# Sparse first FFN: what GpSimd does between its sends, and the tick at which the expert blocks begin

## The chip, the core and the metric

The kernel runs on one core of a Trainium2 chip. The metric is the device time in microseconds (us), lower is better. Three runs of the kernel before gave 2142.99, 2148.42 and 2147.09 us (median 2147.09).

The core has these engines, each with its own in-order program: TensorE (PE in the profile; its weight loads are PEld), VectorE (DVE), ScalarE (ACT), GpSimd (POOL) and SyncE (SP), which here only issues DMAs. They wait for each other by semaphores.

## The reference, cut to what matters

The input is eight rows (sequences) of 1024 tokens with 256 numbers each. Three parts follow one another, each added to `x`:

```python
x = x + 0.5 * ffn(layernorm(x))      # first FFN: the part that is changed
x = x + attention(layernorm(x))      # light windows of 64 and 256 heavy tokens
x = x + 0.5 * ffn(layernorm(x))      # second FFN, dense in this kernel

def ffn(x):                          # 8 experts, two for each token
    logits = x @ router_w + router_b
    w, idx = top_k(softmax(logits), 2);  w = w / sum(w)
    h = gelu(x @ W1[e] + b1[e])      # 256 -> 128, for each expert e
    y = h @ W2[e] + b2[e]            # 128 -> 256
    return sum over the token's two experts of w * y
```

With two experts the normalized weights depend only on the difference of the two largest logits: with t = exp(second - first), they are 1/(1+t) and t/(1+t).

## The kernel before, in words

The first FFN is sparse. Each row is routed; every token's normalized 256 numbers are sent by two scattering DMAs to spots in DRAM (`spots_d`), so that the tokens of one expert lie together; then blocks of 256 tokens are loaded, run through one expert's two products, and stored (`made_d`). Attention's first steps fetch the results back. Rows are taken in three batches, (0, 1), (2, 3, 4) and (5, 6, 7), with 23, 31 and 31 blocks, 85 in all. A batch's blocks need all of its rows sent and a table of its counts.

All five engine programs of this stage run over the same ticks `tau`; a tick is no clock, it is only the order in which each engine takes its work. `ROW_AT` gives each row the tick at which it begins, `STEP0` the tick of block 0, and block s is at tick `STEP0 + s`. A row's stages, by ticks after its start:

- 0 and 1, DVE: `bn_stats` and `bn_aggr` of the two halves (`row_stats`, needs the row's load)
- 2, POOL: the norm factors (`row_rstd`), four operations, one of them a power
- 3 and 4, ACT: the normalization in place (`row_norm`, L1127)
- 4 to 7: turning on PE (L816), copies on ACT (L1136), logits on PE (L826), copies on ACT (L1143), turning the logits (L833)
- 8, DVE: ranks of the experts (`row_route`, L1422 to L1443)
- 9, PE: counts before each token (L841, L843). 9, POOL: exp of the difference by a power (`row_exp`, L1915)
- 10, DVE: the spots (`row_spots`, L1476), the batch's table after its last row, and the two gates (`row_gates`)
- 11 to 16, POOL: 16 indirect DMAs (`send`, L1923), 128 tokens of 1 KB each

A block's stages: load by SP three ticks ahead (L604, into one of four buffers `xin`, so a load waits until the block four before it has been turned), at its tick the turning on PE (L853), the copy of its expert's W1 (L1164) and the copy `xh` (L1149) on ACT; one tick later the first product (L862), two later Gelu (L1170), three later the second product (L877), four later the bias add on DVE (L1538), five later the store (L610). Before the first block of a batch SP writes eight pads of zeros (`pads`, L592, 256 KB each), and waits for the batch's sends and for the pads to land.

There are four buffers `xb` for rows: the load of row r (`row_load`, L585) is issued five ticks ahead of the row and waits until row r-4 has been sent. SP also writes spare zeros for each batch (L652, 7 x 256 KB) at ticks 12, 40 and 64. Attention's preparation of row 0 (fetching, norms, turning) is tied to `ROW0 = STEP0 + FIRST[2] + 1`, where `FIRST[2]` is 54, and runs beside the blocks of the last batch. `made`, `sent` and the stores' semaphores close the stage; attention follows, unchanged.

Of the kernel before, what the change touches and what calls it, by code (L numbers as in the profile page):

```python
# [18 lines left out]
P = 128  # L19
# [19 lines left out]
def build(nc, x_in, gamma_h, wq_h, wkv_h, wo_h, ln_g, ln_b, wqkv, wo_l, rt_q, rt_kv,  # L39
# [30 lines left out]
    with ctx:  # L70
# [111 lines left out]
        half_a, euler_a = sb("half_a", [P, T]), sb("euler_a", [P, T])  # L182
        st_a, mv_a = sb("st_a", [P, T, 6]), sb("mv_a", [P, T, 2])
        vt_a, rs_a, nm_a = sb("vt_a", [P, T]), sb("rs_a", [P, T]), sb("nm_a", [P, T])
        chosen = [sb(f"chosen{i}", [P, T + 1, E], BF16) for i in range(2)]
        lg = sb("lg", [P, T, E])
        lmax_a, t2nd_a, wt_a = sb("lmax_a", [P, T]), sb("t2nd_a", [P, T]), sb("wt_a", [P, T])
# [89 lines left out]
        s_abn, s_amv, s_avar, s_ars, s_arstd, s_anorm = sem("a_bn"), sem("a_mv"), sem("a_var"), sem("a_rs"), sem("a_rstd"), sem("a_normed")  # L277
        s_ax, s_lq, s_ra, s_exa, s_pos, s_tab, s_zero = sem("xa_turned"), sem("logits_left"), sem("route_a"), sem("exp2_a"), sem("spots"), sem("table"), sem("pads")
        s_home, s_b2all, s_xa0 = sem("homes"), sem("b2_all"), sem("xa_ld_first")
# [37 lines left out]
        STEP0 = 26  # L317
        TICKS = STEP0 + STEPS + 6
        ROW_AT = (0, 6, 12, 19, 26, 36, 46, 56)
# [217 lines left out]
        NA, NPOS, NTAB = 14, 6, 16  # L537
# [36 lines left out]
        def sp_program():  # L574
# [60 lines left out]
            for tau in range(TICKS):  # L635
                for s_ in step_at(tau - 5):
                    block_store(s_)
                for s_ in step_at(tau + 3):
                    block_load(s_)
                for r in row_at(tau + 5, 0):  # L640
                    if r >= 4:
                        row_load(r)
                if tau == 8:
                    sp.dma_start(wqkv_st[:, :, :], wqkv.rearrange("(c p) n -> p c n", p=P)).then_inc(s_wld[4], 16)
                if tau == 10:
                    sp.dma_start(b2_all[:, :, :].rearrange("p e n -> p (e n)"), b2.rearrange("(a e) n -> a (e n)", a=1).broadcast_to([P, E * D])).then_inc(s_b2all, 16)
                if tau in (12, 40, 64):

                    if tau == 12:
                        sp.wait_ge(s_const, CONST)  # L650
                    n = (12, 40, 64).index(tau)
                    sp.dma_start(spots_d[n][SPARE[n]:SPARE[n] + (E - 1) * BLK, :].rearrange("(j p s) d -> p j (s d)", p=P, s=BT),  # L652
                                 zeros[:, :, :].rearrange("p s d -> p (s d)").unsqueeze(1).broadcast_to([P, E - 1, BT * D])).then_inc(s_spare, 16)
                if tau == 18:

                    sp.wait_ge(s_wlo, 6)
                    sp.dma_start(w1_d, w1_s[:, :, :, :, :].rearrange("p e w c f -> p (e w c f)").bitcast(F32)).then_inc(s_wst, 16)
                    for n in range(2):
                        sp.dma_start(w2_d[n], w2_s[n][:, :, :].rearrange("p e n -> p (e n)").bitcast(F32)).then_inc(s_wst, 16)
                    sp.dma_start(b2_d, b2_s[:, :].bitcast(F32)).then_inc(s_wst, 16)  # L660
                if tau == 74:
                    attn_load(0, x_v)
                if tau == 100:
                    sp.dma_start(wqh_s[:, :, :], wq_h.rearrange("(c p) n -> p c n", p=P)).then_inc(s_late, 16)
                    sp.dma_start(wol_s[:, :, :], wo_l.rearrange("(c p) n -> p c n", p=P)).then_inc(s_late, 16)
                if tau == 106:
                    sp.dma_start(wkvh_s[:, :, :], wkv_h.rearrange("(c p) n -> p c n", p=P)).then_inc(s_late, 16)
                    sp.dma_start(woh_s[:, :, :], wo_h.rearrange("(c p) n -> p c n", p=P)).then_inc(s_late, 16)
# [400 lines left out]
        def act_program():  # L1069
# [52 lines left out]

            def row_norm(r, h):
# [195 lines left out]
            for tau in range(TICKS):  # L1319
                for s_ in step_at(tau - 2):  # L1320
                    block_gelu(s_)
                for s_ in step_at(tau):
                    w1_copy(s_)
                    block_x(s_)
                for h in range(2):
                    for r in row_at(tau, 3 + h):
                        row_norm(r, h)
                for what in tick_jobs(tau):
                    evac(*what)
# [10 lines left out]
                if 14 <= tau < 14 + 2 * 3 * C and tau % 2 == 0:  # L1340
                    i, n = (tau - 14) // 2 % C, (tau - 14) // 2 // C * INNER
                    split(wqkv_s[0][:, i, n:n + INNER], wqkv_st[:, i, n:n + INNER], (s_wld[4], 16))
# [33 lines left out]
        def dve_program():  # L1376
# [22 lines left out]
            def row_stats(r, h):  # L1399
# [9 lines left out]
                if h == 0 and r > 0:  # L1409
                    dve.wait_ge(s_avar, 2 * r)  # L1410
# [4 lines left out]
            def row_route(r):  # L1415
# [25 lines left out]
                dve.tensor_reduce(t2nd_a[:, :], l2nd[:, :, :], AX_X, ALU.add).then_inc(s_ra)  # L1441
                dve.wait_ge(s_ra, n + 10)
                dve.tensor_tensor(t2nd_a[:, :], t2nd_a[:, :], lmax_a[:, :], ALU.subtract).then_inc(s_ra)  # L1443

            def row_gates(r):
                n = NA * r
                dve.wait_ge(s_exa, r + 1)
                g = share[:, r, :, :]
                dve.tensor_scalar(wt_a[:, :], t2nd_a[:, :], 1.0, 2.0, ALU.add, ALU.mult).then_inc(s_ra)
                dve.wait_ge(s_ra, n + 12)  # L1450
                dve.reciprocal(g[:, 0, :], wt_a[:, :]).then_inc(s_ra)
                dve.wait_ge(s_ra, n + 13)
                dve.tensor_tensor(g[:, 1, :], t2nd_a[:, :], g[:, 0, :], ALU.mult).then_inc(s_ra)
# [319 lines left out]
            for tau in range(TICKS):  # L1773
                for s_ in step_at(tau - 4):
                    block_left(s_)
                for h in range(2):
                    for r in row_at(tau, h):
                        row_stats(r, h)
                for r in row_at(tau, 10):
# [3 lines left out]
                    row_gates(r)  # L1783
# [13 lines left out]
                if 15 <= tau < 15 + 2 * 3 * C and tau % 2 == 1:  # L1797
                    m = (tau - 15) // 2
# [50 lines left out]
        def pool_program():  # L1849
# [49 lines left out]
            def row_rstd(r):  # L1899

                pool.wait_ge(s_amv, 2 * r + 2)
                if r > 0:
                    pool.wait_ge(s_anorm, 4 * r)
                    pool.wait_ge(s_arstd, r)
                pool.tensor_scalar(vt_a[:, :], mv_a[:, :, 1], LN_EPS, None, ALU.add).then_inc(s_avar)
                pool.tensor_scalar(nm_a[:, :], mv_a[:, :, 0], -1.0, None, ALU.mult).then_inc(s_avar)
                pool.wait_ge(s_avar, 2 * r + 1)
                pool.tensor_tensor(rs_a[:, :], vt_a[:, :], half_a[:, :], ALU.pow).then_inc(s_ars)
                pool.wait_ge(s_ars, r + 1)
                pool.wait_ge(s_avar, 2 * r + 2)  # L1910
                pool.tensor_tensor(nm_a[:, :], nm_a[:, :], rs_a[:, :], ALU.mult).then_inc(s_arstd)
# [71 lines left out]
            pool.memset(half_a[:], -0.5)  # L1983
            pool.memset(euler_a[:], float(np.e))
# [30 lines left out]
            for tau in range(TICKS):  # L2015
                for r in row_at(tau, 2):
                    row_rstd(r)
                for r in row_at(tau, 9):
                    row_exp(r)
# [93 lines left out]
```

## Time and profile before

| what | us |
|---|---|
| median of three runs | 2147.09 |
| the profiled execution's own time | 2143.95 |
| its span | 2142.2 |
| PE busy | 1899.1 (89% of the span) |
| DVE busy | 1389.8 (65%) |
| ACT busy | 1175.3 (55%) |
| POOL busy | 1126.9 (53%) |
| SP's load of row 1 for attention, behind the last block's store, at | 417.7 |

The page's slices of 53.6 us each show the first FFN in the first eight: PE is busy there 3 to 8 tenths, and 8 or more tenths in nearly all that follow. The granted TensorE clock is below full speed in the first seven of them.

```profile
PE   4377877968998998998998998998999999999998
PEclk8678988989999999999999999999999999999999
DMA  8557576611031031031031031030023111111110
```

### The profile page before, as it was taken

The page shows a single profiled execution, that of the slowest core. Times are in us where ns is not written, and L with a number is a line of the kernel's source. Part 1 is how long each engine was busy: PE and PEld are TensorE (multiplying, and loading weights), DVE is VectorE, ACT ScalarE, POOL GpSimd, SP SyncE. Part 2 cuts the span into 40 slices and gives each one's busy share as a digit, 9 for nine tenths or more (in the row PEclk, how much of TensorE's full clock was granted, in tenths as well). Part 3 has the DMA queues.
Part 4 walks back from the last instruction along what each step waited for, and adds up shares of the span by engine and source line. Part 5 has one row for each costly group of instructions (what it writes and reads, how often), then busy time and mean ns, then how long its engine had stood idle before and what let it go on. Part 6 is the DMA issues. An engine that isn't in the chain of part 4 may idle for free.

```text
span 2142.2 us, 37969 instructions
## 1 busy us (share of the span) xinstructions
PE 1899.1 (89%) x11764; PEld 1409.7 (66%) x11764; DVE 1389.8 (65%) x4781; ACT 1175.3 (55%) x2936; POOL 1126.9 (53%) x1253
## 2 busy tenths in 40 slices
PE   4377877968998998998998998998999999999998
PEld 2155566845665666665665665665676688888887
DVE  5343344476586585685685685685664488888887
ACT  4244444645557556556556556656555555555554
POOL 5745434157277277377376386386354444444444
PEclk8678988989999999999999999999999999999999
DMA  8557576611031031031031031030023111111110
GB/s 291 194 170 260 197 255 231 233 57 33 1 94 40 1 97 38 1 97 38 1 102 33 1 104 31 3 105 28 1 58 116 37 33 38 40 41 39 36 36 30
DMA packets 106575, 173.64 MB, mean 81 GB/s; under 512 B 13296, under 2 KB 64904, under 8 KB 105480
## 3 DMA queue, kind: packets, MB, share of 16 engines
q1 hardware_dynamic: 83336, 118.42, 16.7%
q0 software_dynamic: 20736, 52.52, 7.8%
q8 instruction: 97, 1.59, 0.3%
q14 instruction: 102, 0.84, 0.1%
q10 hardware_dynamic: 2304, 0.28, 0.1%
HBM read 80.33 MB, written 90.84 MB: 80 GB/s over the span
## 4 chain that ended last, share of the span: by engine, by line
PE 46%; DVE 16%; issue 13%; POOL 12%; ACT 8%; DMA 2%; another core or an unknown queue 1%; SPq 1%; DVEq 0%; ACTq 0%; POOLq 0%
PE bank L720 6%; PE bank L722 5%; PE bank L721 5%; PE bank L1009 4%; PE bank L998 4%; PE bank L969 4%; PE bank L980 4%; PE bank L940 3%; POOL spots_d L1923 3%; ACT prob L1292 2%; POOL prob L1970 2%; DVE x L1550 2%; DVE st L1381 2%; PE bank L971 1%; PE bank L877 1%
## 5 line engine op out<-in xcount | busy, mean ns | idle before, releaser
L1970 POOL TENSOR_TENSOR prob<-prob,rden 128x512 f32<-128x512 f32 x320 | 337.2, 1055 | 452.7 <-DVE rden L1756 449.1
L1292 ACT ACTIVATE prob<-prob,nmax 128x256 f32<-128x256 f32 x512 | 256.0, 502 | 401.8 <-DVE nmax L1738 393.4
L1738 DVE CUSTOM_DVE_ANT_0 prob<-bank,mask 128x256 f32<-128x256 f32 x512 | 195.4, 418 | 105.0 <-PE bank L969 103.5
L1625 DVE SCALAR_TENSOR_TENSOR xb<-bank,gate,xb 128x256 f32<-128x256 f32 x512 | 211.9, 477 | 55.6 <-PE bank L722 55.1
L969 PE MATMUL bank<-kT,qT 64*128 64x256 f32 x1024 | 213.2, 434 | 22.2 <-DVE nmax L1738 21.6
L1885 POOL TENSOR_TENSOR hl<-hf,hh 128x512 fp32r<-128x512 f32 x128 | 164.6, 1291 | 113.9 <-ACT hh L1109 109.2
L980 PE MATMUL bank<-ident,prob 128*128 128x128 f32 x1280 | 199.3, 279 | 20.7 <-POOL prob L1970 20.7
L980 PEld LDWEIGHTS bank<-ident,prob 128*128 128x128 f32 x1280 | 153.9, 142 | 79.9 <-POOL prob L1970 33.3
L1750 DVE COPY probT<-bank 128x512 f32<-128x512 f32 x160 | 110.2, 688 | 117.5 <-PE bank L980 116.6
L1108 ACT ACTIVATE hf<-bank,b1s 128x512 f32<-128x512 f32 x128 | 88.2, 689 | 171.2 <-PE bank L722 167.7
L998 PE MATMUL bank<-probT,V 128*64 128x128 f32 x2048 | 170.7, 288 | 9.1 <-ACT oT_s L1308 7.7
L1538 DVE TENSOR_TENSOR yout<-bank,b_all 128x512 f32<-128x512 f32 x85 | 58.0, 690 | 174.4 <-remote 71.5
L1957 POOL DMA_INDIRECT hs_d<-yr,place x128 | 129.8, 1014 | 44.5 <-issue 32.8
L969 PEld LDWEIGHTS bank<-kT,qT 64*128 64x128 f32 x1024 | 94.9, 188 | 86.5 <-issue 48.2
L998 PEld LDWEIGHTS bank<-probT,V 128*64 128x64 f32 x2048 | 108.8, 137 | 64.4 <-issue 61.0
L1923 POOL DMA_INDIRECT spots_d<-xb,spot x128 | 125.2, 978 | 48.1 <-issue 36.3
L720 PE MATMUL bank<-w,hh 128*128 128x256 f32 x512 | 146.4, 286 | 3.8 <-POOL hl L1885 2.7
L722 PE MATMUL bank<-w,hh 128*128 128x256 f32 x512 | 144.8, 283 | 0.0
L721 PE MATMUL bank<-w,hl 128*128 128x256 f32 x512 | 144.4, 282 | 0.0
L1009 PE MATMUL bank<-wol,oT_s 128*128 128x256 f32 x512 | 126.3, 390 | 1.2 <-ACT xf_t L1239 1.2
L1770 DVE TENSOR_TENSOR x<-bank,x 128x256 f32<-128x256 f32 x64 | 27.1, 423 | 145.3 <-PE bank L1009 145.3
L877 PE MATMUL bank<-w_st,hf 128*128 x340 | 97.0, 411 | 21.3 <-issue 13.6
(254 smaller groups left out, 5016.7 us busy)
## 6 DMA issues: line engine op xcount, KB each, us to landing
xin<-spots_d SPq DMA_DIRECT2D x85, 256.0 KB
made_d<-yout SPq DMA_DIRECT2D x85, 256.0 KB
x<-in_L_attn_x SPq DMA_DIRECT2D x8, 1024.0 KB
x_d<-x SPq DMA_DIRECT2D x8, 1024.0 KB, 4.4
xb<-x_d SPq DMA_DIRECT2D x16, 512.0 KB, 3.8
out<-xb SPq DMA_DIRECT2D x16, 512.0 KB, 2.9
xb<-in_L_attn_x SPq DMA_DIRECT2D x7, 1024.0 KB
spots_d<-zeros SPq DMA_DIRECT2D x24, 256.0 KB
```

The lines of the kernel that those rows point to most:

```text
L720: pe.matmul(o, w[0], x[0], start=start, stop=False)
L721: pe.matmul(o, w[1], x[0], start=False, stop=False)
L722: return pe.matmul(o, w[0], x[1], start=False, stop=stop)
L969: ins = pe.matmul(bank[g % NS][:, 0:KEYS], qT[hs, hp, t * P:(t + 1) * P], kT[hs, hp, t * P:t * P + KEYS], start=True, stop=True)
L980: ins = pe.transpose(bank[3 + j % 2][:, (2 * h + kk) * P:(2 * h + kk + 1) * P], prob[j % NP][:, h, kk * P:(kk + 1) * P], ident[:, :])
L998: ins = pe.matmul(bank[5][h * DH:(h + 1) * DH, hp * P:(hp + 1) * P], V[:, t + kk, hs] if t < T else hv[:, kk, hs], probT[j % 2][:, 2 * h + ...
L1009: ins = pe.matmul(bank[tb][:, 0:D], oT_s[:, ch, :], w[:, ch, :], start=(ch == 0), stop=(ch == HC - 1))
L1292: act.activation(prob[j % NP][:, h, :], src, ACT.Exp, bias=nmax[:, j % 4, h:h + 1], scale=-1.0 if light else 1.0, accum_out=den[:, j % 4, ...
L1625: dve.scalar_tensor_tensor(out=x, in0=bank[ob][:, (t % 2) * D:(t % 2 + 1) * D], scalar=gate[:, k % 2, t, e:e + 1], in1=x, op0=ALU.mult, op ...
L1738: ins = dve.tensor_tensor_reduce(prob[j % NP][:, h, :], bank[g % NS][:, 0:KEYS], mask[:, which, :], -1.0, 3e38, ALU.add, ALU.min, nmax[:, ...
L1923: pool.indirect_dma_start(spots_d[batch_of_row(r)], bass.IndirectOffsetOnAxis(spot[:, r, c, t:t + 1], 0), xb[r % 4][:, t, :], None).then_i ...
L1970: pool.tensor_tensor(prob[j % NP][:, :, :], prob[j % NP][:, :, :], rden[:, j % 4, :].unsqueeze(2).broadcast_to([P, 2, KEYS]), ALU.mult).th ...
```

## The change

1. `row_rstd` moves from POOL to ACT: one `Ln` with bias eps and one `Exp` with scale -0.5 give the factor; the shift is one operation on DVE (`row_shift`).
2. `row_exp` and `row_gates`, once for each row, become one `Exp` over all rows on ACT at tick 51 (`share_exps`) and three operations on DVE at tick 52 (`shares`). The first combine of attention waits for them.
3. POOL then has nothing between its sends.
4. Rows begin every six ticks, and block 0 is at tick 44 (before: 26), two ticks after row 7 has begun. Loads for attention move from ticks 74, 100, 106 to 94, 120, 126; the splits of `wqkv` are at every tick instead of every second one.

```diff
-        STEP0 = 26
+        STEP0 = 44
-        ROW_AT = (0, 6, 12, 19, 26, 36, 46, 56)
+        ROW_AT = (0, 6, 12, 18, 24, 30, 36, 42)
+        SHARES = ROW_AT[-1] + 9
-        NA, NPOS, NTAB = 14, 6, 16
+        NA, NPOS, NTAB = 11, 6, 16
...
+            def row_rstd(r):
+                act.wait_ge(s_amv, 2 * r + 2)
+                act.activation(ln_a[:, :], mv_a[:, :, 1], ACT.Ln, bias=eps_a[:, 0:1]).then_inc(s_aln)
+                act.wait_ge(s_aln, r + 1)
+                if r > 0:
+                    act.wait_ge(s_arstd, r)
+                act.activation(rs_a[:, :], ln_a[:, :], ACT.Exp, scale=-0.5).then_inc(s_ars)
+            def share_exps():
+                act.wait_ge(s_ra, NA * ROWS)
+                act.activation(t2nd_a[:, :, :], t2nd_a[:, :, :], ACT.Exp).then_inc(s_exa)
...
+                for r in row_at(tau, 2):
+                    row_rstd(r)
...
+                if tau == SHARES:
+                    share_exps()
...
-            def row_gates(r):
-                dve.wait_ge(s_exa, r + 1)
...
+            def row_shift(r):
+                dve.wait_ge(s_ars, r + 1)
+                if r > 0:
+                    dve.wait_ge(s_anorm, 4 * r)
+                dve.scalar_tensor_tensor(out=nm_a[:, :], in0=mv_a[:, :, 0], scalar=-1.0, in1=rs_a[:, :], op0=ALU.mult, op1=ALU.mult).then_inc(s_arstd)
+            def shares():
+                dve.wait_ge(s_exa, 1)
+                dve.tensor_scalar(wt_a[:, :, :], t2nd_a[:, :, :], 1.0, 2.0, ALU.add, ALU.mult).then_inc(s_share)
...
+                    dve.wait_ge(s_share, 3)
...
-            def row_rstd(r):
-                pool.wait_ge(s_amv, 2 * r + 2)
...
-                pool.tensor_tensor(rs_a[:, :], vt_a[:, :], half_a[:, :], ALU.pow).then_inc(s_ars)
...
-            def row_exp(r):
-                pool.wait_ge(s_ra, NA * r + 11)
-                pool.tensor_tensor(t2nd_a[:, :], euler_a[:, :], t2nd_a[:, :], ALU.pow).then_inc(s_exa)
```

What the change does to the order of the engines shows at three places: GpSimd's sends, SyncE ahead of the first block, and TensorE and ScalarE at block 0. On GpSimd before, from the first row's sends on (`xb_194` and the numbers after it are the row buffers; a number at the end counts equal operations):

```order
L1915 TENSOR_TENSOR t2nd_a<-euler_a,t2nd_a 128x8
L1923 DMA spots_d<-xb_194,spot 20224x256 x9
L1905 TENSOR_SCALAR vt_a<-mv_a 128x8
L1906 TENSOR_SCALAR nm_a<-mv_a 128x8
L1908 TENSOR_TENSOR rs_a<-vt_a,half_a 128x8
L1911 TENSOR_TENSOR nm_a<-nm_a,rs_a 128x8
L1923 DMA spots_d<-xb_194,spot 20224x256 x3
```

and now, where the row buffers are `xb_193` to `xb_196`:

```order
L1934 DMA spots_d<-xb_193,spot 20224x256 x16
L1934 DMA spots_d<-xb_194,spot 20224x256 x16
L1934 DMA spots_d<-xb_195,spot 28416x256 x16
L1934 DMA spots_d<-xb_196,spot 28416x256 x16
L1934 DMA spots_d<-xb_193,spot 28416x256 x16
L1934 DMA spots_d<-xb_194,spot 28416x256 x16
L1934 DMA spots_d<-xb_195,spot 28416x256 x16
L1934 DMA spots_d<-xb_196,spot 28416x256 x16
```

The eight operations on norm factors and exps that stood between the sends of each row are gone, and the 128 sends stand in one piece.

On SyncE before, from the load of row 4 to the first block's load:

```order
L585 DMA xb_194<-in_L_attn_x 128x8x256 [waits sent0]
L714 TENSOR_LOAD pad_row_179 [waits table]
...
L592 DMA spots_d<-zeros 128x512
L714 TENSOR_LOAD block_row_176 [waits pads,spare_zero,sent1,sent0]
L604 ISA
L604 DMA xin_164<-spots_d 128x512
```

and now:

```order
L586 DMA xb_193<-in_L_attn_x 128x8x256 [waits sent0]
L586 DMA xb_194<-in_L_attn_x 128x8x256 [waits sent1]
L586 DMA xb_195<-in_L_attn_x 128x8x256 [waits sent2]
L586 DMA xb_196<-in_L_attn_x 128x8x256 [waits sent3]
L653 DMA spots_d<-zeros 128x7x512
L715 TENSOR_LOAD pad_row_178 [waits table]
...
L593 DMA spots_d<-zeros 128x512
L715 TENSOR_LOAD block_row_175 [waits pads,spare_zero,sent1,sent0]
L605 ISA
L605 DMA xin_163<-spots_d 128x512
```

The loads of rows 5, 6 and 7 and the second batch's spare zeros have moved ahead of the first batch's pads and of every block's load.

On TensorE now, around block 0 (`xin_163` is its load, `chosen_133` belongs to row 6):

```order
L834 MATMUL bank<-ident,lgT_167 128x8 x4
L834 MATMUL bank<-ident,lgT_168 128x8 x4
L854 MATMUL bank<-ident,xin_163 128x128 x4
L854 MATMUL bank<-ident,xin_164 128x128 x4
L863 MATMUL bank<-xh_198,w_now_189 128x256 x2
L842 MATMUL bank<-chosen_133,later 128x72
L844 MATMUL bank<-chosen_133,ones 128x64
```

Before, in this place row 3 was routed:

```order
L853 MATMUL bank<-ident,xin_164 128x128 x4
L833 MATMUL bank<-ident,lgT_168 128x8 x4
L833 MATMUL bank<-ident,lgT_169 128x8 x4
L853 MATMUL bank<-ident,xin_165 128x128 x4
L862 MATMUL bank<-xh_199,w_now_190 128x256 x2
L853 MATMUL bank<-ident,xin_166 128x128 x4
L862 MATMUL bank<-xh_200,w_now_191 128x256 x2
L841 MATMUL bank<-chosen_135,later 128x72
```

Row 6's counts now stand behind the turning of blocks 0 and 1, and all of row 7's work on TensorE behind that; before, this was so from row 3 on.

On ScalarE now, at tick 44:

```order
L1164 ACTIVATE xh_198<-bank 128x512
L1127 ACT_TABLE_LOAD
L1127 ACTIVATE ln_a<-mv_a,eps_a 128x8
L1131 ACT_TABLE_LOAD
L1131 ACTIVATE rs_a<-ln_a 128x8
```

Row 7's factors stand behind block 0's copy, and each of the eight rows brings two table loads.

## Rows read from the trace of the kernel before

**Rows 1.** Line L1149 (copy `xh`, one a block) by stretches; x counts blocks
```profile
core 0: us, ACT busy (x), PEclk, DMA share, GB/s
86.90:131.20 44.30, 3.54 (x6) 0.77 0.58 191
131.20:160.00 28.80, 4.08 (x7) 0.80 0.38 128
160.00:178.50 18.50, 1.77 (x3) 0.86 0.97 345
178.50:196.50 18.00, 3.51 (x6) 0.91 0.44 149
196.50:221.00 24.50, 1.75 (x3) 0.84 0.85 283
221.00:243.20 22.20, 4.11 (x7) 0.87 0.47 151
243.20:267.30 24.10, 2.33 (x4) 0.93 0.64 218
267.30:278.30 11.00, 2.90 (x5) 1.00 0.78 286
278.30:301.00 22.70, 1.75 (x3) 0.79 0.64 220
301.00:321.70 20.70, 5.28 (x9) 0.90 0.86 272
321.70:328.80 7.10, 0.58 (x1) 0.78 0.50 168
...
348.00:411.70 63.70, 16.42 (x27) 0.99 0.78 259
```

**Rows 2.** GpSimd's groups in the first 320 us
```profile
L1923 POOL DMA_INDIRECT spots_d<-xb,spot x128 | 125.2, 978 | 48.1 <-issue 36.3 <-DVE spot L1476 11.8
L1915 POOL TENSOR_TENSOR t2nd_a<-euler_a,t2nd_a 128x8 f32<-128x8 f32 x8 | 14.2, 1772 | 70.0 <-DVE t2nd_a L1443 69.8
L1908 POOL TENSOR_TENSOR rs_a<-vt_a,half_a 128x8 f32<-128x8 f32 x8 | 13.6, 1706 | 0.0
```

**Rows 3.** GpSimd in order of time: start, duration, what
```profile
35.07 1.23 POOL L1923 DMA_INDIRECT spots_d<-xb,spot  x1 [0.20 <-issue]
...
103.85 0.51 POOL L1905 TENSOR_SCALAR vt_a<-mv_a 128x8 f32<-128x8 f32 x1
...
145.56 1.67 POOL L1915 TENSOR_TENSOR t2nd_a<-euler_a,t2nd_a 128x8 f32<-128x8 f32 x1 [15.53 <-DVE t2nd_a L1443]
```

**Rows 4.** SyncE in order of time
```profile
61.29 0.40 SPq L585 DMA_DIRECT2D xb<-in_L_attn_x  x1
62.41 15.65 SPq L592 DMA_DIRECT2D spots_d<-zeros  x8
86.88 24.71 SPq L604 DMA_DIRECT2D xin<-spots_d  x8
```

**Rows 5.** ScalarE in order of time: copies of blocks 0, 1 and 53, a table load
```profile
90.85 0.58 ACT L1149 ACTIVATE xh<-bank 128x512 f32<-128x512 f32 x1
...
106.72 0.60 ACT L1149 ACTIVATE xh<-bank 128x512 f32<-128x512 f32 x1 [14.98 <-remote]
107.33 1.28 ACT L1170 ACT_TABLE_LOAD   x1
108.63 0.47 ACT L1170 ACTIVATE hf<-bank,b1s 128x256 f32<-128x256 f32 x1
...
322.38 0.58 ACT L1149 ACTIVATE xh<-bank 128x512 f32<-128x512 f32 x1
```

**Rows 6.** VectorE in order of time: spots of row 0, route of row 3
```profile
34.33 0.17 DVE L1476 CAST spot<-spot_f 128x16 uint32<-128x16 f32 x1
...
103.18 0.22 DVE L1422 TENSOR_TENSOR lg<-bank,rbs 128x64 f32<-128x64 f32 x1 [12.63 <-remote]
```

**Rows 7.** TensorE in order of time: the turned logits of row 3
```profile
90.23 0.66 PE L833 MATMUL bank<-ident,lgT 8*128 8x8 f32 x8
```

More of the change, by code:

```diff
@@ L1339, in act_program @@
                         act.activation(b2_s[at_:at_ + E, :], b2_st[:, :], ACT.Copy).then_inc(s_whi)
-                if 14 <= tau < 14 + 2 * 3 * C and tau % 2 == 0:
-                    i, n = (tau - 14) // 2 % C, (tau - 14) // 2 // C * INNER
+                if 14 <= tau < 14 + 3 * C:
+                    i, n = (tau - 14) % C, (tau - 14) // C * INNER
                     split(wqkv_s[0][:, i, n:n + INNER], wqkv_st[:, i, n:n + INNER], (s_wld[4], 16))
@@ L1409, in row_stats @@
                 if h == 0 and r > 0:
-                    dve.wait_ge(s_avar, 2 * r)
+                    dve.wait_ge(s_aln, r)
                 for q in range(TG * h, TG * h + TG):
@@ L1440, in row_route @@
                 dve.wait_ge(s_ra, n + 8)
-                dve.tensor_reduce(t2nd_a[:, :], l2nd[:, :, :], AX_X, ALU.add).then_inc(s_ra)
+                dve.tensor_reduce(t2nd_a[:, r, :], l2nd[:, :, :], AX_X, ALU.add).then_inc(s_ra)
                 dve.wait_ge(s_ra, n + 10)
-                dve.tensor_tensor(t2nd_a[:, :], t2nd_a[:, :], lmax_a[:, :], ALU.subtract).then_inc(s_ra)
-            def row_gates(r):
-                n = NA * r
-                dve.wait_ge(s_exa, r + 1)
[L1448 to L1453, printed above, removed]
+                dve.tensor_tensor(t2nd_a[:, r, :], t2nd_a[:, r, :], lmax_a[:, :], ALU.subtract).then_inc(s_ra)
+            def row_shift(r):
[6 more added lines that the diff above has]
+                dve.tensor_scalar(wt_a[:, :, :], t2nd_a[:, :, :], 1.0, 2.0, ALU.add, ALU.mult).then_inc(s_share)
+                dve.wait_ge(s_share, 1)
+                dve.reciprocal(share[:, :, 0, :], wt_a[:, :, :]).then_inc(s_share)
+                dve.wait_ge(s_share, 2)
+                dve.tensor_tensor(share[:, :, 1, :], t2nd_a[:, :, :], share[:, :, 0, :], ALU.mult).then_inc(s_share)
             def row_spots(r):
@@ L1778, in dve_program @@
                         row_stats(r, h)
+                for r in row_at(tau, 2):
+                    row_shift(r)
+                if tau == SHARES + 1:
+                    shares()
                 for r in row_at(tau, 10):
@@ L1782, in dve_program @@
                         batch_table(batch_of_row(r))
-                    row_gates(r)
                 for r in row_at(tau, 8):
@@ L1796, in dve_program @@
                     split(b2_s[64:64 + E, :], b2_st[:, :], b2_s[0:E, :], 7)
-                if 15 <= tau < 15 + 2 * 3 * C and tau % 2 == 1:
-                    m = (tau - 15) // 2
+                if 15 <= tau < 15 + 3 * C:
+                    m = tau - 15
                     i, n = m % C, m // C * INNER
@@ L2015, in pool_program @@
             for tau in range(TICKS):
[L2016 to L2019, printed above, removed]
                 for i in range(2 * T):
```

28 lines of the change are left out of this document (9 added, 19 removed).

## The prediction

> **What bounds the kernel now.** The first FFN ends at 417.7 us of the span (SyncE's load of row 1 for attention), and everything behind it is unchanged work that starts when the last blocks are done. So the change is worth what it does to that point. I read the slices of the page first: TensorE is busy 89% of the whole span, but in the first eight slices only 3 to 8 tenths, at a granted clock of 0.5 to 0.9. The slack is there. Then I counted blocks: ScalarE's copy L1149 runs once for each block, so its count by stretches is the pace of the pipeline [rows 1]. I cut the stretches where GpSimd starts and stops sending.
>
> In the five stretches in which GpSimd sends while blocks run (those that begin at 86.9, 160.0, 196.5, 243.2 and 278.3) there are 6+3+3+4+3 = 19 blocks in 44.3+18.5+24.5+24.1+22.7 = 134.1 us: 7.06 us a block. In the five between them 7+6+7+5+9 = 34 blocks take 28.8+18.0+22.2+11.0+20.7 = 100.7 us: 2.96 a block with the routing of rows among them, and 2.30 where no row is routed (9 in 20.7, from 301.0). The last stretch has 27 in 63.7, 2.36 [rows 1]. So a block costs three times as much beside sends, and blocks 0 to 53 take from 90.85 to 322.38 [rows 5], 231.5 us.
>
> What stalls there is seen best at the start. Row 3's turned logits are recorded on TensorE at 90.23 [rows 7], yet VectorE, which waits for nothing else, gets them at 103.18 [rows 6]; block 1's copy on ScalarE starts at 106.72 after 14.98 us idle [rows 5]. GpSimd's sends pause at 103.85, for row 4's norm factors [rows 3]. The other slow stretches end within 2 to 3 us of the last send too. I do not know what TensorE waits for; I use only that it goes with sends. The granted clock of 0.77 to 0.86 in these stretches and 0.99 to 1.00 in steady ones [rows 1] follows from the idle time.
>
> **Part by part.** *GpSimd.* It loses 8 x 1.77 = 14.2 us of exps and 8 x 1.71 = 13.6 us of powers and the small operations around them [rows 2]. A send is 0.978 us and 36.3/123 = 0.30 of issue behind it [rows 2], together 1.27, so a row takes 16 x 1.27 = 20.3 us and eight rows 162 us without a pause. The first send waits now for the spots, done at 34.33 + 0.17 = 34.5 [rows 6], instead of the power until 35.07 [rows 3]: 0.4 us, on the path of the sends. Row 3's last send ends at 34.7 + 4 x 20.3 = 116. Row 6 could begin at 34.7 + 6 x 20.3 = 156.
>
> *SyncE.* All rows' loads now stand ahead of the first pads. Row 7's load waits for row 3 sent, 116 and about 1.5 for landing: 117.5. Behind it come 1.0 MB of row, 1.8 MB of spare zeros and 2.1 MB of pads before a block may be loaded. Before, 1.0 + 2.1 MB took from 61.29 to 86.88, 25.6 us [rows 4], part of it waiting for row 1 to be sent. Bounds for the new 4.9 MB: 14 us at 345 GB/s, the highest rate in [rows 1], and 25.6 x 4.9 / 3.1 = 40 us. I take 22 us (some 225 GB/s, between the 191 and 283 of two stretches with sends). Block 0 loads at 139.5 and is copied 4.0 us later, as before (86.88 to 90.85 [rows 4, 5]): 143.5, against 90.85.
>
> *Blocks beside sends.* Rows 0 to 5 are routed by then, row 6 up to its logits. Row 6's counts stand behind the turning of blocks 0 and 1 and one hidden product, and row 7's factors behind block 0's copy. From 143.5 until 156 row 5's sends run; then GpSimd runs dry, TensorE is free of the stall, row 6 is ready near 158. In 14.5 us at 7.06: 2 blocks. Row 6's sends and their tail, 158 to 180: 22/7.06 = 3 blocks. Row 7 is then routed in its last ticks (46 to 52 stand between blocks) and GpSimd idles, as it does now (15.53 us ahead of row 4's exp [rows 3]); I take 10 us, 4 blocks. Row 7's sends, 190 to 212: 3 blocks. So 12 blocks by 212.
>
> *The rest.* 42 blocks to block 53, with no send and no row beside them: 42 x 2.30 = 96.6. The change of batch costs 7.1 - 2.3 = 4.8 (one block in 7.1, from 321.7 [rows 1]). Two table loads around the single exp at tick 51 (Exp in, Gelu back) are 2 x 1.28 [rows 5] = 2.6, of which the slack of ScalarE in a step hides a part: 1.9. Sum 212 + 96.6 + 4.8 + 1.9 = 315.3, against 322.4: 7 us earlier. Bounds of the pace of the 42: 2.17 would be the shortest spacing within the last stretch as a whole (I take 2.2) and 2.96 the mean with rows: 309 to 343.
>
> *At nothing.* The 16 table loads of the rows (two a row, by the order of ScalarE) are 20.5 us of ScalarE, and 14 of them lie in the time in which it waits for sends to free a row buffer; if that cover were gone they would cost 2.6 us a row in the chain of each. Row 0's chain: 4 operations on GpSimd and one table load before, two loads and three small ones now, equal within 1 us. The gates of all rows together are four small operations long before attention's first combine. The wqkv splits at every tick are done before the blocks; so are, by then, all waits on them. The last batch, 322 to 418, keeps its own order of blocks, fetches and loads, and shifts as a whole; if its cover changed it would cost or give what lies in its 19.2 us beside fetches, some 5 us.
>
> One rule weighs against this. [Rows 5] show a table load of 1.28 us, with the activation behind it 1.30 us after its start. The Trainium skill ("ScalarE: Activation LUTs", "What ACT_TABLE_LOAD costs") adds a drain of about 1.38 us to each, 2.66 in all. By it the pair at tick 51 would be 5.3 us and the sum would end about 2.7 us later; the trace does not show the drain, so I keep the row.
>
> Result: the profiled execution's 2143.95 - 7 = 2137; on the median of the runs, 3.1 above it, 2140.
>
> **The rivals.**
>
> *A: sends are not the cause.* The slow stretches also hold loads of rows (1 MB each, ahead of blocks in SyncE's queue), and TensorE's work of a row; these are what goes from the blocks' time. For it: each slow stretch has a row under way. Against: the ends fall on GpSimd's pauses. Then blocks beside sends go at 2.96: 23 by 212, and 31 x 2.3 + 6.7 behind them: 290, 32 us earlier, 2108 on the median. With only half of it 2124.
>
> *B: slower, by a long run of sends.* Before, GpSimd's own norm operations broke the runs (5 us at 103.85, when blocks 1 to 3 slipped through); now nothing does. If TensorE stands while sends run, block 0's late load and the stall hold row 6's counts and row 7's whole chain. Priced: pads at the upper bound, block 0 copied at 158 when GpSimd has run dry; row 6 spots at 163; 1 block beside its sends until 185; row 7's chain then takes 19 us, 6 blocks; its sends until 226, 2 blocks: 10 blocks by 226, 44 x 2.3 + 6.7: 334, 12 us later, 2159 at the outside and 2155 as the case's centre. It decides at 3 blocks fewer than my 12 by 212. A rule gives the same end: by the Trainium skill ("DMA: Bandwidth & Descriptors", "Queues, rings and completion order") a completion is a strongly ordered write that lands only after every earlier write of that DMA engine, across its queues, so block loads would complete behind scattered sends. [Rows 6, 7] show a wait of 13 us that is on no DMA at all, so the rule alone does not cover it.
>
> *C: it does little.* The blocks begin 53 us later and the rest is 2.4 to 2.5 a block because of spare zeros and a second change of buffers: 42 x 0.15 = 6 us more. Then it ends within 0.3%, near 2146.
>
> **How the numbers follow.** My forecast 0.42, A 0.20, B 0.24, C 0.14. The bound of no change is 0.3%, 6.4 us, about what a measurement of this kernel can tell. The forecast's own range is 2128 to 2150, of which 0.28 is faster by more than the bound, 0.12 within it and 0.02 slower. A is faster. C is 0.12 within and 0.02 slower; B 0.02 within and 0.22 slower. Faster 0.48, same 0.26, slower 0.26. The range 2110 to 2158 takes A nearly whole and B to its centre and beyond.
>
> **What would show it right or wrong.** GpSimd's sends stand at 1.27 us apart from 34.7 to 156 without a gap, then a gap of some us before row 6 and one of about 10 before row 7, the last send near 210. The first block load at 139.5 (135 to 155). L1149's count is about 9 between 143 and 190 and 12 by 212, then one each 2.3 us at a clock near 1.0. Row 7's first norm is behind block 0's copy. Block 53 is copied near 315, attention's load of row 1 near 411. Twenty-one table loads instead of four, and no time behind 411 that differs. I am wrong in the mechanism if blocks beside sends go at 3 us, or if the stretch behind the last send has gaps of its own; in the size, if the first load is far from 139.5 or row 7's gap far from 10.

## The result and the profile after

The changed kernel takes 2182.36 us (median of 4 runs, 2180.86 to 2184.63), against 2147.76 for the kernel before, timed beside it: a ratio of 1.0163, interval 1.0141 to 1.0185. It is 35 us slower; the forecast was 7 us faster, with 2110 to 2158 as its range. The profiled execution took 2182.36, its span 2180.6.

From the page, the span and two of the slices' rows (columns as before):

```profile
span 2180.6 us, 37947 instructions
...
PE   3335787978899898998999998998999999999998
...
PEclk8657799989999999999999999999999999999999
```

TensorE is busy 3 to 5 tenths in the second to fourth slice (55 to 218 us), where it was 3 to 7 before. The count of blocks tells more. Copies of blocks on ScalarE (L1164 now, L1149 in [rows 1]) by stretches, cut again where GpSimd starts and stops sending:

```profile
core 0: us, ACT busy (x), PEclk, DMA share, GB/s
37.00:79.30 42.30, 0.00 (x0) 0.66 0.61 223
79.30:94.00 14.70, 0.00 (x0) 0.50 0.24 80
94.00:134.40 40.40, 0.00 (x0) 0.58 0.37 127
134.40:153.10 18.70, 0.00 (x0) 0.59 0.78 273
153.10:186.10 33.00, 0.00 (x0) 0.68 0.35 120
186.10:253.70 67.60, 7.13 (x12) 0.79 0.49 162
253.70:276.00 22.30, 5.60 (x10) 0.87 0.71 225
276.00:294.00 18.00, 1.98 (x4) 0.81 0.86 304
294.00:355.50 61.50, 16.19 (x28) 1.00 0.77 250
355.50:385.00 29.50, 2.95 (x5) 0.78 0.69 227
385.00:446.90 61.90, 15.89 (x26) 0.99 0.80 257
```

The 12 blocks beside sends are there, but by 253.7 us instead of 212. Behind them block 53 is copied at 355.5, so the stretch with no send took 101.8 us, where my sum had 103.3. Between 294.0 and 355.5 a block takes 61.5/28 = 2.20 us. The loss has been made by the time the last send is out, and measured by my forecast it all lies ahead of block 0: from block 0's copy at 186.1 to the last send the 12 blocks take 67.6 us, where my forecast had 68.5 (143.5 to 212).

GpSimd in order of time: where rows' sends stop and start, and its group in the first 320 us ([rows 2, 3] are the same of before):

```profile
36.95 1.27 POOL L1934 DMA_INDIRECT spots_d<-xb,spot  x1 [30.04 <-DVE spot L1501]
...
78.30 0.96 POOL L1934 DMA_INDIRECT spots_d<-xb,spot  x1 [0.30 <-issue]
93.99 0.96 POOL L1934 DMA_INDIRECT spots_d<-xb,spot  x1 [14.73 <-DVE spot L1501]
...
133.38 0.96 POOL L1934 DMA_INDIRECT spots_d<-xb,spot  x1 [0.30 <-issue]
153.08 0.96 POOL L1934 DMA_INDIRECT spots_d<-xb,spot  x1 [18.74 <-DVE spot L1501]
...
233.45 0.95 POOL L1934 DMA_INDIRECT spots_d<-xb,spot  x1 [11.66 <-DVE spot L1501]
```

```profile
L1934 POOL DMA_INDIRECT spots_d<-xb,spot x128 | 125.9, 983 | 120.8 <-DVE spot L1501 83.6 <-issue 37.2
```

A send is what it was (0.983 us and 0.29 of issue). But GpSimd now waits 83.6 us for spots, 30.04 of them ahead of row 0. The other 53.6 are five gaps between rows (14.7, 18.7, 4.1, 4.3 and 11.7 us), and I had put two there, together 12 us. Before, it waited 11.8 us for spots and 69.8 for what its exps read [rows 2], nearly as long, and had 34 us of own work besides. The engine that was to be relieved stands still, because the rows are not routed.

Why not, row 2 shows. ScalarE in order of time: it copies row 2's turned tiles (L1151) and logits (L1158), then makes row 3's factors:

```profile
53.30 0.60 ACT L1151 ACTIVATE xa<-bank 128x512 f32<-128x512 f32 x1 [1.47 <-PE bank L817]
56.88 0.60 ACT L1151 ACTIVATE xa<-bank 128x512 f32<-128x512 f32 x1 [2.98 <-remote]
...
61.15 0.60 ACT L1151 ACTIVATE xa<-bank 128x512 f32<-128x512 f32 x1 [3.15 <-remote]
66.09 0.60 ACT L1151 ACTIVATE xa<-bank 128x512 f32<-128x512 f32 x1 [4.35 <-PE bank L827]
...
75.27 0.59 ACT L1158 ACTIVATE lgT<-bank 8x512 f32<-8x512 f32 x1 [8.07 <-remote]
83.01 0.59 ACT L1158 ACTIVATE lgT<-bank 8x512 f32<-8x512 f32 x1 [7.15 <-remote]
...
84.65 1.28 ACT L1127 ACT_TABLE_LOAD   x1
85.94 0.30 ACT L1127 ACTIVATE ln_a<-mv_a,eps_a 128x8 f32<-128x8 f32 x1
86.26 1.28 ACT L1131 ACT_TABLE_LOAD   x1
```

TensorE in order of time, the logits of row 2 and their turning:

```profile
61.89 3.39 PE L827 MATMUL bank<-xa,rw_st 128*8 128x512 f32 x4 [3.18 <-issue]
66.84 1.88 PE L827 MATMUL bank<-xa,rw_st 128*8 128x512 f32 x4 [1.56 <-issue]
83.65 1.02 PE L834 MATMUL bank<-ident,lgT 8*128 8x8 f32 x8 [14.93 <-ACT lgT L1158]
```

TensorE's last logits product is done at 68.7 by the record; ScalarE, idle, copies it at 83.01. The trace also records each update of a semaphore. For the six groups of row 2, the end of the matmul that increments the semaphore and the time at which the semaphore moved (us, from the trace's records, not from a view of the page):

```
matmul ends   semaphore moves   behind   ScalarE starts
  52.26           53.28           1.02       53.30
  53.17           56.86           3.69       56.88
  55.13           61.12           5.99       61.15
  58.71           66.07           7.36       66.09
  65.27           75.25           9.98       75.27
  68.71           82.98          14.27       83.01
```

ScalarE starts 0.02 to 0.03 us behind each update. TensorE itself goes on: ScalarE's copy of 66.09 is done at 66.69, and the matmuls that need it start at 66.84, 8.4 us before the increment of the group ahead of them moves (75.25). What is late is TensorE's increment, and the later the longer GpSimd has been sending without a break; the last send of this run starts at 78.30. In the same stretch (37 to 254 us) 80 updates by ScalarE's own instructions are recorded, none more than 0.1 us behind its end; of TensorE's 72, 31 are. This is what [rows 5 to 7] showed without a name: a product recorded at 90.23 and received at 103.18.

### The profile page after: what moved, and what is told of

Read it like the earlier page. It is cut to its first block, busy times and chain, and to the rows that moved or that the text cites. A ratio compares the mean times of both kernels' runs of the same rounds, so it can differ in the third digit from the quotient of the medians.

```text
span 2180.6 us, 37947 instructions
## 1 busy us (share of the span) xinstructions
PE 1898.9 (87%) x11764; PEld 1412.9 (65%) x11764; DVE 1389.5 (64%) x4768; ACT 1203.1 (55%) x2970; POOL 1094.4 (50%) x1212
## 4 chain that ended last, share of the span: by engine, by line
PE 50%; DVE 16%; issue 13%; ACT 8%; POOL 8%; DMA 3%; another core or an unknown queue 1%; SPq 1%; ACTq 0%; DVEq 0%; POOLq 0%
PE bank L721 6%; PE bank L723 5%; PE bank L722 5%; PE bank L1010 4%; PE bank L999 4%; PE bank L970 4%; PE bank L981 3%; PE bank L878 3%; PE bank L941 3%; PE bank L863 3%; ACT prob L1307 2%; POOL prob L1981 2%; DVE x L1576 2%; DVE st L1400 1%; PE bank L972 1%
## 5 line engine op out<-in xcount | busy, mean ns | idle before, releaser
L1934 POOL DMA_INDIRECT spots_d<-xb,spot x128 | 125.9, 983 | 120.8 <-DVE spot L1501 83.6
L999 PEld LDWEIGHTS bank<-probT,V 128*64 128x64 f32 x2048 | 108.7, 137 | 64.4 <-issue 60.9
L721 PE MATMUL bank<-xt_hi,wqkv_hi 128*128 128x512 f32 x256 | 114.8, 448 | 0.0
```

Source lines behind the costliest of these rows:

```text
L721: pe.matmul(o, w[0], x[0], start=start, stop=False)
L999: ins = pe.matmul(bank[5][h * DH:(h + 1) * DH, hp * P:(hp + 1) * P], V[:, t + kk, hs] if t < T else hv[:, kk, hs], probT[j % 2][:, 2 * h + ...
```

## The experiments

In what follows "late" counts, while sends run, TensorE's increments that land over 0.1 us behind the latest matmul that could have made them. It is a lower bound: a queue of increments can hide part of it. Some updates are missing from each trace (one of TensorE's semaphores has 545 for 568 matmuls in the changed kernel). Where sends are called a run, no other operation of GpSimd and no gap lies between them. An increment is put to the last send that started before it landed, if that was at most 4 us before.

### One part of the change at a time

**ticks_only**: the kernel before, with the new numbers.

```diff
-        STEP0 = 26
+        STEP0 = 44
-        ROW_AT = (0, 6, 12, 19, 26, 36, 46, 56)
+        ROW_AT = (0, 6, 12, 18, 24, 30, 36, 42)
```

(and SyncE's three late loads 20 ticks later, as in the change)

> The kernel before with only the numbers of ticks changed (blocks begin at tick 44, rows at 0, 6, 12, 18, 24, 30, 36, 42; the norm factors and exps stay on GpSimd). Theory 1, the late start is the cost: few blocks run beside the sends, as in the changed kernel (14 by 259 us against 36 before), so the stage is 25 to 40 us longer and the time 2172 to 2190. Theory 2, GpSimd's lost work is the cost (its norm operations broke the runs of sends and let the next row's routing through): with them back the rows are routed faster and the time is within 0.5% of the kernel before, 2140 to 2158. In both, TensorE's semaphore increments land late beside sends (up to 14 us in the changed kernel).

Measured: 2162.56, ratio 1.0065 (1.0048 to 1.0082), 14 us slower than before and 20 faster than the changed kernel. It lies between the two theories. The sends end at 233 (253 in the changed kernel) although GpSimd has 34 us more to do. GpSimd in this run, around the factors of row 3:

```profile
72.22 0.96 POOL L1923 DMA_INDIRECT spots_d<-xb,spot  x1 [0.30 <-issue]
73.26 0.25 POOL L1905 TENSOR_SCALAR vt_a<-mv_a 128x8 f32<-128x8 f32 x1
...
73.80 1.67 POOL L1908 TENSOR_TENSOR rs_a<-vt_a,half_a 128x8 f32<-128x8 f32 x1
...
75.92 1.07 POOL L1923 DMA_INDIRECT spots_d<-xb,spot  x1 [0.17 <-issue]
...
79.56 1.67 POOL L1915 TENSOR_TENSOR t2nd_a<-euler_a,t2nd_a 128x8 f32<-128x8 f32 x1
81.42 1.03 POOL L1923 DMA_INDIRECT spots_d<-xb,spot  x1 [0.19 <-issue]
```

The increments of TensorE's matmuls that end at 78.05, 79.03, 81.54 and 82.39, just behind the two breaks, land within 0.02 us. The rows' sends then start 25 us apart (33.9, 60.9, 86.6, 111.0, 136.1, ...), with a single longer gap, 9.7 us between two sends' starts, at 199. The work that the change takes off GpSimd was what let the routing through.

**engine_only**: the changed kernel, with the old numbers (the reverse of the diff above).

> The changed kernel with the ticks of before (blocks from tick 26, rows at 0, 6, 12, 19, 26, 36, 46, 56): GpSimd only sends, ScalarE makes factors and gates. Theory 1 (the late start is the cost): 2125 to 2150, no slower than before, since blocks run beside the sends again and the sends end up to 28 us earlier. Theory 2 (the unbroken sends are the cost): 2165 to 2185, with gaps of 10 us and more between the rows' sends as in the changed kernel.

Measured: 2159.02, ratio 1.0050 (1.0032 to 1.0068), 11 us slower than before. So neither theory alone: late start 14 us, GpSimd's breaks 11 (with ScalarE's table loads and splits, which this kernel has too), and the remaining 9 to 10 of the 35 only with both. From row 2 on, a row's first send starts 12, 12, 15, 26, 27 and 25 us behind the last one of the row before; the last send is at 310.0, later than the 297.5 of before. Of the increments that land from the sixth send of a run on, 51 of 53 are late, up to 15.6 us; at the first to fifth 1 of 18. Blocks by stretches (L1164), with sends and without:

```profile
102.40:313.00 210.60, 25.81 (x44) 0.86 0.62 204
313.00:424.40 111.40, 24.12 (x40) 0.92 0.77 249
```

### What holds the increments

**pause_each**: the changed kernel; the edit is behind the send in `send`, twice:

```diff
+                pool.wait_ge(s_idle, idles[0])
+                pool.tensor_tensor(idle_b[:, :], euler[:, :], euler[:, :], ALU.pow).then_inc(s_idle)
+                idles[0] += 1
```

> The changed kernel with two small powers on GpSimd behind each send, so that sends stand some 3 us apart instead of 1.27. If TensorE's increments are held by sends that come back to back, they land within 1 us now, no row waits for its spots behind TensorE, and blocks beside sends go at 2.2 to 3.5 us instead of 7; the stage is then bound by GpSimd, 128 sends at 3 us, and the whole is some 2250 to 2350. If it is each send that costs TensorE a fixed time, the increments are as late per send as now: a block beside sends takes the time of one or two sends and more, and the time is longer still.

Measured: 2299.07, sends 3.4 us apart. All 183 increments that land in the time of the sends are in time, 43 of them while a send is under way, and blocks 0 to 53, all beside sends, go at 2.7 us each. So a send by itself costs TensorE nothing; only sends in a run do.

**plain_send**: each send a plain transfer by the same engine. The blocks read a buffer whose rows are not sorted, so the output is another.

```diff
-                pool.indirect_dma_start(spots_d[batch_of_row(r)], bass.IndirectOffsetOnAxis(spot[:, r, c, t:t + 1], 0), xb[r % 4][:, t, :], None).then_inc(s_sc[r % 4], 16)
+                pool.dma_start(plain_d[(16 * r + i) * P:(16 * r + i + 1) * P, :], xb[r % 4][:, t, :]).then_inc(s_sc[r % 4], 16)
```

> The changed kernel with each send a plain transfer of the same 128 x 1 KB by GpSimd, to a buffer of its own, instead of an indirect one (blocks then read that buffer: the rows are not sorted by expert, so the result is another). If the indirect addressing is what holds TensorE's increments, they are on time (under 0.1 us) and blocks beside sends go at 2.2 to 3 us. If it is any transfer whose descriptors GpSimd writes, or the bytes, they stay late by up to 14 us and the stage is like that of the changed kernel.

Measured: 2093.42, with sends 0.53 us apart. Between 35 and 169 us 90 increments of TensorE land and none is late. But 16 such sends are out in 8.5 us, and indirect ones hold nearly every increment only from the sixth, over 6 us into a run. Time and form were not told apart; plain_double, below, does it.

**plain_double**: plain_send, with a second transfer ahead of each (128 x 1 KB from a tile of zeros, to a buffer of its own).

```diff
+                pool.dma_start(extra_d[(16 * r + i) * P:(16 * r + i + 1) * P, :], zeros[:, 0, :]).then_inc(s_extra, 16)
```

> plain_send with every send preceded by a second plain transfer of the same size, from a tile of zeros to a buffer of its own, so that GpSimd issues 32 transfers a row, 0.54 us apart, in runs of 17 us. In plain_send the runs were 16 long and 8.5 us, and of the increments that landed beside them none was late, but indirect sends hold increments only from the sixth of a run, 7.6 us in: time and number are not told apart. If it is the time for which GpSimd issues without a break, increments are late here by several us from 8 us into a run, as beside indirect sends. If it is the indirect form, none is late even at 17 us.

Measured: 2120.61. The rows came so close together that the first run is 96 transfers in 51 us; GpSimd at its end:

```profile
86.59 0.54 POOL L1939 DMA_DIRECT2D extra_d<-zeros  x1
87.12 0.54 POOL L1940 DMA_DIRECT2D plain_d<-xb  x1
```

Of the 96 increments between 37 and 205 us none is later than 0.02 us. It is the indirect form, not GpSimd's issuing without a break, and not these bytes: more of them were moved here in less time. Which part of the indirect form does it (the work on the indices, of which a send's 0.96 us against 0.54 is a sign, or the scattered places) no run separates. The few late increments of this kernel (up to 10 us) lie at 314 to 326 us, where GpSimd fetches row 0 of attention, by index.

### How long a run may be

All of these have one or two idle powers (1.04 us each) behind some sends, by `if i % 4 == 3:` or the like around the edit of pause_each.

**pause4_late**: the changed kernel, two powers behind every fourth send.

> The changed kernel with two idle powers (2 x 1.04 us) on GpSimd behind every fourth send. By the theory that runs of indirect sends hold TensorE's increments, the rows are routed in time: a row takes 16 x 1.27 + 4 x 2.3 = 29.5 us without gaps beside, sends end near 37 + 8 x 29.5 = 273, about 20 us later than in the changed kernel, but blocks beside them go at 3 us, not 7: 2155 to 2180. By the theory that GpSimd's total time is what counts, it is slower than the changed kernel by its 67 us of pauses less the 54 us of gaps: 2185 to 2200.

Measured: 2150.77, ratio 1.0023 (1.0009 to 1.0038): 32 us faster than the changed kernel, by nothing but 67 us of useless work on GpSimd. The last send is 15 us later (267.6), but 26 blocks are done by then and not 12; no increment beside sends is over 2.5 us late. No row waits for its spots any more: between rows GpSimd stands no longer than its pause (2.3 to 2.6 us), where the changed kernel had gaps of up to 18.7. It was even better than the first theory said, by 4 us.

**pause4_early**, **pause4_early_short**, **pause2_early**: engine_only with two powers behind every fourth send, with one behind every fourth, with one behind every second.

> The changed kernel with the ticks of before (as engine_only) and two idle powers behind every fourth send. Theory of held increments: no increment later than 1 us, blocks beside sends at 3 us instead of 7, sends end near 275 with 55 blocks or more done (44 by 310 in engine_only), block 84 copied 20 to 50 us sooner than in engine_only: 2100 to 2140. Rival (blocks beside sends are slow by the transfers' bandwidth): like engine_only or slower by the pauses, 2155 to 2200.

> As pause4_early with one idle power (1.04 us) behind every fourth send. If what matters is that a backlog of the sends drains, and this pause drains too little, some increments are late again and the time is between engine_only and pause4_early, 2130 to 2155; if any break is enough, it is 8 x 4 x 1.1 = 35 us of GpSimd shorter than pause4_early and faster by up to 15 us: 2090 to 2130.

> As pause4_early with one idle power behind every second send: the same sum of pauses, spread. If the length of a run counts, it is as fast as pause4_early or up to 10 us faster; if the length of a pause counts, it is slower and increments are late again.

Measured: 2105.86 (0.9800, 0.9769 to 0.9830), 2094.06 (0.9746, 0.9716 to 0.9776) and 2103.40 (0.9801, 0.9774 to 0.9827). All three times are as a branch of their expectations had them; of pause4_early's details two were missed: increments are up to 1.9 us late (at most 1 expected), and 51 blocks are done by the end of the sends (55). The length of the break hardly counts, its cost does. With one power, increments are 2.3 us late at most beside sends, and the sends end at 258.8 with 49 blocks done (44 by 310.0 in engine_only). The rival, that the bandwidth makes these blocks slow, is out.

Between pause4_late and pause4_early only the ticks differ: 44.9 us. Without the stall, that is what it costs to leave TensorE without blocks until 178 us.

**before_pause4**: the kernel before with one power behind every fourth send.

> The kernel before (GpSimd keeps norm factors and exps) with one idle power (1.04 us) on GpSimd behind every fourth send. Theory of held increments: before had 49 increments over 0.5 us late, up to 14; with runs of at most four sends none is over 3, and it is 30 to 50 us faster than before, 2095 to 2120, while it still loses to pause4_early_short (2094) by GpSimd's 28 us of own work as far as the sends set the pace: 2100 to 2115. Rival (only ScalarE's factors with pauses gain): 2140 or more.

Measured: 2107.04, ratio 0.9804 (0.9769 to 0.9839). So the move of factors and gates to ScalarE is worth 13 us (2107.04 to 2094.06; the intervals of the two ratios just touch) once the runs are broken, and costs 11 as long as they are not.

**drain4**: no idle work; GpSimd waits until all sends before have landed.

```diff
+                    if r > 0:
+                        pool.wait_ge(s_sc[(r - 1) % 4], 32 * T * ((r - 1) // 4 + 1))
+                if i > 0 and i % 4 == 0:
+                    pool.wait_ge(s_sc[r % 4], 32 * T * (r // 4) + 16 * i)
```

> engine_only with no idle work: GpSimd waits at every fourth send, and at a row's first, until all sends before have landed. A send issued at 78.3 had its last packet at 80.3 in the changed kernel, so a break is about 2 us: 8 x 4 x 2 = 64 us of breaks, like pause4_early. If an empty GpSimd (and not what it does in the break) is what lets increments through, 2095 to 2115, as pause4_early (2106) or a little better. If only idle work on the engine did it, 2150 or more, as engine_only (2159).

Measured: 2125.01, ratio 0.9887 (0.9849 to 0.9926). 34 us better than engine_only, with no increment over 2.1 us late: the break works, whatever GpSimd does in it. My number was missed by 10 us. Beside block loads a send takes longer to land than I had read: breaks make gaps of 2.7 to 7.7 us between sends' starts, and the last send is at 299.5.

**rows_sooner**: pause4_early_short with `ROW_AT = (0, 6, 12, 19, 26, 33, 40, 47)`.

> pause4_early_short with rows at ticks 0, 6, 12, 19, 26, 33, 40, 47 (the last three 3, 6 and 9 ticks sooner). There, rows 5 to 7 left gaps of 6, 15 and 11 us between sends. If these gaps cost, sends end up to 25 us sooner and the time is 5 to 15 us less, 2080 to 2090; if blocks give back at 2.2 us each what they lose to earlier sends, it is the same within 0.3%, 2088 to 2100.

Measured: 2091.64, ratio 0.9744 (0.9707 to 0.9782), no different from 2094.06. The sends end at 234.3 instead of 258.8, with 41 blocks done instead of 49, and block 53 is copied at 268.5 in one and 268.7 in the other. The second branch was right.

**fetch_pause**: pause4_early_short with a power behind every fourth of the 16 fetches for row 0 of attention too.

> pause4_early_short with the same idle power behind every fourth of GpSimd's sixteen fetches for row 0 of attention, which also run 1.27 us apart beside blocks. If they hold TensorE's increments as sends do, 3 to 8 us less: 2086 to 2091. If reads by index do no such thing, no change, or 0 to 2 us more.

Measured: 2085.70, ratio 0.9709 (0.9676 to 0.9743), the fastest of all: 3% under the kernel before. Its interval overlaps that of pause4_early_short, but the traces put the gain where the new breaks are: block 53 is copied at 269.6 (268.7 there), block 84 at 351.6 (359.0). In pause4_early_short increments at 294 us were up to 7.5 us late, beside the fetches; here none is over 1.4 there. Reads by index do the same as writes. GpSimd, and blocks (L1166) by stretches, the first two beside sends:

```profile
85.98 0.96 POOL L1936 DMA_INDIRECT spots_d<-xb,spot  x1 [0.30 <-issue]
86.96 1.04 POOL L1939 TENSOR_TENSOR idle_b<-cols 128x4 f32<-128x4 f32 x1
88.20 1.03 POOL L1936 DMA_INDIRECT spots_d<-xb,spot  x1 [0.20 <-issue]
```

```profile
93.00:163.00 70.00, 11.84 (x20) 0.92 0.82 277
163.00:261.90 98.90, 17.59 (x30) 0.95 0.82 272
```

50 blocks in 168.9 us with five rows routed among them, 3.4 us each, where engine_only took 210.6/44 = 4.8; DMA moves 272 to 277 GB/s instead of 204.

**pause8_early**: fetch_pause with the sends' power behind every eighth.

> fetch_pause with the sends' idle power behind every eighth send instead of every fourth (the fetches keep theirs). GpSimd has 16 x 1.1 = 18 us less to do in eight rows. Since held increments begin at the third send of a run and reach 3 to 14 us from the sixth on, runs of eight should bring back part of the stall: 2095 to 2125, slower than fetch_pause (2086). If a break of one power is enough for any run, it is as fast or up to 10 us faster, 2076 to 2088.

Measured: 2135.41, ratio 0.9943 (0.9926 to 0.9961): 50 us slower than fetch_pause, for 18 us less of idle work, and 10 us beyond the range I gave. Increments are up to 12.1 us late again, and ahead of rows 5 to 7 sends start 25 us apart again. So a break of one power does not undo a run of eight: even at the first two sends behind it increments are up to 7.2 us late. Four is short enough, eight is not; between them nothing was run.

## Why the prediction was wrong

- **Sends at 1.27 us without a gap from 34.7 to 156.** This is the step that failed. Their rate was right; that a row's spots would always be ready was not. Row 3 was sent at 134.3 instead of 116, and five gaps of together 53.6 us stand in the row of sends: 37.5 of them ahead of rows 2, 4 and 5, where I had none, and 16.0 ahead of rows 6 and 7, where I had 12. I had taken the stall for something that costs blocks, and priced it so (7.06 us a block), but let the routing of rows 1 to 6 go on beside it for nothing. It runs over the same semaphores of TensorE. So the sends choke what they wait for: rows 2 and 4 had their spots only when the row before was out and GpSimd had stood for 14.7 and 18.7 us. pause4_late, which only breaks the runs, has none of these gaps.
- **GpSimd's lost work, 27.8 us.** The 13.6 us in it are the powers alone; the three small operations around them are 2.3, 2.2 and 1.6 us more, 34 in all. No term of the sum hung on it, as little as on the clock in the page's first slices, 0.6 to 0.9 and not 0.5 to 0.9.
- **Late start.** By the old pace a block beside sends seemed to be worth little, 19 in 134 us, so I let them go cheaply: 12 by 212. ticks_only puts the start's share at 14 us, and it is 45 where TensorE is hardly held.
- **Block 0's load at 139.5, copied 4 us later.** SyncE, in order of time:

```profile
61.44 74.75 SPq L586 DMA_DIRECT2D xb<-in_L_attn_x  x4
136.24 0.58 SPq L653 DMA_DIRECT2D spots_d<-zeros  x1
138.37 7.95 SPq L593 DMA_DIRECT2D spots_d<-zeros  x8
152.87 50.35 SPq L605 DMA_DIRECT2D xin<-spots_d  x8
```

  Row 7's load went out at 135.8, and from there to the first block load are 17.0 us, where I had taken 22 (117.5 to 139.5). The 13 us are the sends' again. The 4 us were wrong as well, by 29: the block waited for TensorE, whose program has row 6's turning and logits ahead of it.

```profile
168.79 1.09 PE L817 MATMUL bank<-ident,xb 128*128 128x128 f32 x4
176.62 2.95 PE L817 MATMUL bank<-ident,xb 128*128 128x128 f32 x12 [6.73 <-DVE picks L1497]
...
185.10 1.09 PE L854 MATMUL bank<-ident,xin 128*128 128x128 f32 x8
```

- **12 blocks beside the late sends:** 12, in 67.6 us instead of 68.5, but by 253.7. **42 blocks, the change of batch and the tables, 103.3 us:** 101.8. The sum is right by luck. The change from batch 0 to 1 takes 18.0 us for 4 blocks, 9.2 more than plain ones and not 4.8; the plain ones go at 2.20, not 2.30; and the two table loads around the single exp are at 229 and 231 us, ahead of row 7's sends and among the 12 blocks, so their 1.9 us did not belong here.
- **At nothing.** The 16 table loads of the rows are there, 1.28 us each, with the activation 1.29 to 1.30 us behind the start of each (84.65 to 85.94), so the drain that the Trainium skill adds ("ScalarE: Activation LUTs", "What ACT_TABLE_LOAD costs") does not show here either. Whether they cost a chain 2.6 us was not run by itself: ticks_only, which has none, differs in more than these. Behind 355.5 the kernel is 5 us longer than before behind 322.4 (1825.1 against 1819.8 us of span), of which I had none. SyncE's load of row 1 for attention goes out at 453.1, 97.5 us behind block 53's copy, against 95.3 before (417.7), so 2 us are in the last batch and 3 in attention and behind. Their cause stays open; the median differs by 35, the profiles by 38.
- **The rivals.** A is out: the transfers and the rows' work are all there in pause4_early_short. Its price was also wrong by its own sum: 32 us earlier than 2147 is 2115, and I had taken them off my forecast of 2140. C is out: the time is 35 us off, not within 0.3%. B named the mechanism, that an unbroken run of sends starves TensorE and holds the rows' chains, and the side on which it ends. It was priced too low: it had the stall act from row 6 on, with the last send at 226, and it acts from row 2 on, with the last at 253.6. Had I worked out what a stall of 14 us does to each row's chain, of which [rows 3] had the pauses and [rows 5, 6] the size, it would have come first.
- **The rule on completions** that I weighed with B ("DMA: Bandwidth & Descriptors", "Queues, rings and completion order" of the Trainium skill) speaks of DMA completions behind earlier writes. What is late here are increments by matmuls, which are no DMA's, and it has no word on these. The case has nothing by which to judge the rule itself.

## What to carry to other kernels

- An operation on a busy engine can be of use by being there. Before work is moved off an engine, ask what goes on elsewhere during its pauses; a break of 1 us each four indirect DMAs was worth 65 us here, and the whole "relief" was worth 13 us only with it.
- When a consumer idles on "remote" or "issue" while its producer's record has long ended, compare the producer's end with the time at which the semaphore moved. If the semaphore is late, look at what another engine does in that time, and put a break into it: one experiment tells.
- A stall that is found must be charged to every chain that uses the stalled engine, the one that feeds the staller first of all.

## What the runs showed of the hardware

TensorE's semaphore increments land late beside a run of GpSimd's indirect DMAs (128 rows of 1 KB, 1.27 us apart): in the kernel before and in engine_only 5 of 56 at the first to fifth of a run, then 96 of 102, by up to 14 to 16 us. Most of those still held when a run ends land together: in engine_only up to seven within 0.4 us, 2.4 to 3.0 us behind the end of the run's last send. Runs of four with one operation of 1.04 us behind them keep it at 3 us or less; runs of eight let it grow to 12. In the same two kernels no increment by ScalarE (149 and 164 updates) or by VectorE (207 and 203) is late; in the changed kernel 3 of VectorE's 151 are, by up to 4.5 us, which was not followed up. Plain DMAs of the same size by GpSimd, 0.53 us apart and 96 in a row, do nothing of the kind. Why TensorE above all, and what the two share, stays open. So does whether the increment or the end of the matmul is late, since the ends are modelled; that later matmuls start on time (66.84, above) speaks for the increment, and no run here measures it otherwise.
